# Two softmax attentions: eight PSUM banks shared out as 3, 4 and 1 in place of 4, 3 and 1

## The chip, the cores and the metric

One core of a Trainium2 chip runs the whole program in one launch. The metric is device time in microseconds (us): from the start to the end of one execution. Engines have short names: PE is TensorE (its matmuls), PEld is TensorE loading weights, DVE is VectorE, ACT is ScalarE, POOL is GpSimd, SP issues the DMAs.

## The reference, cut to what matters

The input x is (4, 512, 256) in fp32. Eight layers follow one another, each as `x = x + layer(layernorm(x))`. Two of them are softmax attentions with 16 heads of 16 channels; the other six (experts, two linear attentions, choosing experts) are not touched.

```python
def first_attention(x):                       # layer 1
    q, k, v = heads(x @ Wq.T), heads(x @ Wk.T), heads(x @ Wv.T)
    p = softmax(q @ k.T / sqrt(16))           # 512 x 512 for each head
    return merge(p @ v) @ Wo.T

def last_attention(x):                        # layer 7, causal
    ck = layernorm(x @ Wd.T) * gamma + beta   # 64 latent channels
    s = (heads(x) @ absorbed) @ ck.T / sqrt(16)
    p = softmax(where(query >= key, s, -inf))
    return merge(p @ (ck @ Wuv.T)) @ Wo.T
```

## The kernel before

**The work.** Both attentions are one function, `softmax_attention`. It has a prologue for the first batch entry and a loop of four turns, one for each batch entry. A turn has four head groups hg of four heads j; a group has four steps kt, one for each 128 keys. Scores are computed twice. The first pass (`scores`, L603) puts 128 queries on the partitions, so that DVE can take the maximum over the keys (`maximum`: L617, or L613 with the causal mask). The maxima are then folded into q (`negate_max`, `turn_max`, `put_max`). The second pass (`scores_t`, L724) puts 128 keys on the partitions and all queries on the 512 columns; ACT takes the exponential straight from PSUM (L840), and `values` (L739) multiplies by v. In step kt of group hg PE does the second pass of group hg and, in between, the first pass of the next group. In the causal attention matmuls, maxima and exponentials get narrower with kt or query tile, and POOL zeroes the masked corner of the exponentials (L915) before `values` may read them.

**Short names.** s0 to s3 are the first-pass scores of the four heads in a step, t0 to t3 the transposed ones, e0 to e3 their exponentials, V is `values` of the step before. A dash (t0') is the next step's. PE's order in a step is t0 t1, s3, V, s0, t2 t3, s1, [extras], s2. The extras belong to the finished group: its sums of exponentials in step 1 (`denominators`, L750) and its turned reciprocals in step 2 (`turn_reciprocals`, L759); group 2 has also the next entry's turned x and, in the causal layer, the latent projection. After the last step come the q and k of a later group (`qk`, eight passes or four), `turn_max` and V.

**TensorE.** An fp32 matmul is two passes over its columns. A score matmul has 32 rows (one head), so the four heads use four row groups of the array and can run side by side. V, `qk` and the extras use all 128 rows, and begin when the row groups have drained. PE takes its instructions in order: one that waits for a semaphore holds up all behind it.

**Banks.** Eight PSUM banks are handed out by rings (class `Ring`): whoever fills a ring's next bank waits on its `free` semaphore until the bank's last reader is done. Ring A has banks 0 to 3: q, k, v and the transposed scores. These are filled and read in pairs, and one exponential reads two banks (1024 columns). Ring D has banks 4 to 6: first-pass scores, the turned maxima, sums, reciprocals, turned x and latent tiles. Ring O has bank 7 for V's sum. The output projection writes into banks 2 and 3 (`y_banks`) at a turn's end; the wait on `y_free`, before v tile 2 of the next turn, is until DVE has added them to x.

So, when rings have n banks, a score may be filled when the one n places before it in the ring has been read.

Of the kernel before, what the change touches and what calls it, by code (L numbers as in the profile page):

```python
# [22 lines left out]
ACT = mybir.ActivationFunctionType  # L23
# [6 lines left out]
P = 128  # L30
B, T, DM = 4, 512, 256
NT = T // P
KD = DM // P
# [523 lines left out]
HG, HJ, DH, HP = 4, 4, 16, 32  # L557
# [3 lines left out]
def softmax_attention(nc, c, loads, w, causal):  # L561
# [4 lines left out]
    sb = c.carve(c.back, c.n7 if causal else c.n1)  # L566
    qs = sb("qs", [P, HG, T])
    ks = sb("ks", [P, HG, T])
# [3 lines left out]
    pt = sb("pt", [P, 4, 2, T])  # L572
# [5 lines left out]
    head_rows = [slice(j * HP, (j + 1) * HP) for j in range(HJ)]  # L578
# [1 line left out]
    first_slot = c.small[:, c.at["first_slot"]:c.at["first_slot"] + HJ]  # L580
    ones_row = c.small[:, c.at["ones_row"]:c.at["ones_row"] + 1]
    A, D, O = c.A, c.D, c.O
    D.take(c.banks[4:7])
    O.take(c.banks[7:8])
    max_uses = NT * HJ + 1
    y_banks = c.banks[2:4]

    def qk(pe, it, hg):
        pe.wait_ge(A.free.s, A.may_fill(it, 2))
# [3 lines left out]
    def keep_qk(act, it, hg):  # L593
        act.wait_ge(A.full.s, A.may_read(it, 2))
        nc.scalar.activation(qs[:, hg, :], A.read("q", hg)[:], ACT.Identity)
        nc.scalar.activation(ks[:, hg, :], A.read("k", hg)[:], ACT.Identity, bias=ones_row)\
            .then_inc(A.free.s, 2)
# [36 lines left out]
        bank = D.read("turn", hg)  # L634
        nc.vector.tensor_tensor(qs[:, hg, :], qs[:, hg, :], bank[:], ALU.add).then_inc(D.free.s, 1)  # L635

    A.open(4)
    D.open(w.extra_uses + max_uses, whole=False)
    c.first_step.open(w.links)
    c.max_ready.open(1)  # L640
# [2 lines left out]
    with nc.Block() as block:  # L643
        @block.tensor
        def _(pe):
            pe.wait_ge(c.s_small.s, 16)
            w.wait_weights(pe)
            pe.wait_ge(c.set_up.s, c.set_up.at(0, 2))
            pe.wait_ge(D.free.s, D.all_free(0))
            w.project_latent(pe, 0)  # L650
            w.turn_latent(pe, 0)
            qk(pe, 0, 0)
            qk(pe, 0, 1)
            pe.wait_ge(A.free.s, A.released(0, "k", 0))
            for qi in range(NT):
                for j in MAX_ORDER:
                    scores(pe, 0, 0, qi, j)
            turn_max(pe, 0, 0, 1)
            pe.wait_ge(A.free.s, A.released(0, "k", 1))
            pe.wait_ge(D.free.s, D.released(0, "turn", 0))  # L660
# [37 lines left out]
    c.y_free.base += 1  # L698
    c.y_full.open(2)
    c.y_free.open(2)  # L700
    A.open(NT + HG * (2 + NT * HJ))
    D.open(KD + w.extra_uses + HG * (max_uses + 2))
    O.open(HG)
    c.xn_ready.open(1)
    c.max_ready.open(HG)
# [5 lines left out]
    with nc.Block() as block:  # L711
        @block.tensor
        def _(pe):
            with pe.Fori(0, B) as it:
                def v_tile(i):
                    pe.wait_ge(A.free.s, A.may_fill(it))
                    w.v(A.fill("v", i)[:, 0:DM], i).then_inc(A.full.s, 1)

                def scores_t(hg, kt, pair):
                    q0 = kt * P if causal else 0  # L720
                    pe.wait_ge(A.free.s, A.may_fill(it, 2))
                    for j in (2 * pair, 2 * pair + 1):
                        bank = A.fill("s", hg, kt, j)
                        mm = nc.tensor.matmul(bank[:, q0:T], ks[head_rows[j], hg, kt * P:(kt + 1) * P],  # L724
                                              qs[head_rows[j], hg, q0:T], start=True, stop=True)
                    mm.then_inc(A.full.s, 2)

                def values(hg, kt):
                    q0 = kt * P if causal else 0
# [33 lines left out]
                def project(i, groups):  # L763

                    for hg in groups:
                        mm = nc.tensor.matmul(y_banks[i // 2][:, (i % 2) * DM:(i % 2 + 1) * DM],
                                              os_[:, hg, i * P:(i + 1) * P], w.wo[:, hg, :],
                                              start=(hg == 0 and i % 2 == 0), stop=(hg == HG - 1),
                                              skip_group_check=True)
                    return mm  # L770
# [12 lines left out]
                        w.turn_latent(pe, it)  # L783

                for i in range(NT):
                    if i == 2:
                        pe.wait_ge(c.y_free.s, c.y_free.at(it, 0))
                    v_tile(i)
                for hg in range(HG):
# [27 lines left out]
                for i in range(NT):  # L817
                    mm = project(i, range(HG - 1, HG))
# [5 lines left out]
        @block.scalar  # L824
        def _(act):
            with act.Fori(0, B) as it:
                for i in range(NT):
                    act.wait_ge(A.full.s, A.may_read(it))
                    bank = A.read("v", i)
                    nc.scalar.activation(v[:, i, :, 1:1 + DH], bank[:, 0:DM].rearrange("p (h d) -> p h d", d=DH),  # L830
                                         ACT.Identity).then_inc(A.free.s, 1)
                for hg in range(HG):
                    for kt in range(NT):
                        q0 = kt * P if causal else 0
                        for pair in range(2):
                            act.wait_ge(A.full.s, A.may_read(it, 2))
                            A.read("s", hg, kt, 2 * pair)
                            A.read("s", hg, kt, 2 * pair + 1)
                            two = c.a_pair[(A.r - 2) % 4 // 2]
                            nc.scalar.activation(pt[:, (kt % 2) * 2 + pair, :, q0:T], two[:, :, q0:T], ACT.Exp,  # L840
                                                 scale=0.25).then_inc(A.free.s, 2)
                    keep_qk(act, it, (hg + 2) % HG)
                    act.wait_ge(O.full.s, O.may_read(it))
                    bank = O.read("o", hg)
                    nc.scalar.activation(os_[:, hg, :], bank[:], ACT.Identity).then_inc(O.free.s, 1)
# [80 lines left out]
    if causal:  # L926
        c.sum_ready.close()
        c.kt_ready.close()
    c.set_up.base += 2


class MhaWeights:
# [10 lines left out]
    def memory(self, sb):  # L943
        pass
# [35 lines left out]
def mha_layer(nc, c, loads):  # L980
    softmax_attention(nc, c, loads, MhaWeights(nc, c), causal=False)
# [1108 lines left out]
class MlaWeights:  # L2090
# [21 lines left out]
    def memory(self, sb):  # L2112
        self.absorbed = sb("absorbed", [P, 512])
        self.ck = sb("ck", [P, NT, P])
        self.ct = sb("ct", [P, T])
        self.scratch = sb("scratch", [P, 3, T])
        self.spare = self.c.pool_spare

    def wait_weights(self, pe):
# [66 lines left out]
def mla_layer(nc, c, loads):  # L2186
    softmax_attention(nc, c, loads, MlaWeights(nc, c), causal=True)
# [265 lines left out]
```

## Time and profile before

| | us |
|---|---|
| median of 3 runs | 3036.81 (3034.34 to 3045.38) |
| the profiled execution | 3037.58 |
| its span, first to last instruction | 3035.7 |
| the first attention's loop, four turns | about 390 |
| the last attention's loop, four turns | about 398 |

Over the span PE is busy 91%, PEld 64%, DVE 52%, POOL 33% and ACT 29%. A busy PE is not a PE at its peak: a matmul's record covers its latency, and four row groups side by side count once. So the share of busy time doesn't tell whether the two loops could be shorter; the waits inside them do. The granted clock is a share of 2.4 GHz: 1.00 is that level, 0.50 is 1.2 GHz, and a stretch with both has a mean between. The record's own ends of matmuls are modelled, so the argument below goes by starts: weight loads are the sharpest marks on PE.

### The profile page before, as it was taken

Reading aid. Unit: us, or ns where it says so; the run is one execution under the profiler, and the core shown is the slowest. Engines: PE = TensorE matmul, PEld = TensorE weight load, DVE = VectorE, ACT = ScalarE, POOL = GpSimd, SP = SyncE. Lnnn points to the kernel's source line nnn. Section 1 sums busy time; section 2 is a strip of 40 time slices with the busy share of each in tenths; the row PEclk is TensorE's granted clock in tenths of the full one; section 3 lists DMA queues with packets and bytes.
Section 4 is the critical chain, followed back from the end, with each engine's and each line's share of the span. In section 5 each row is a group of like instructions: output and inputs, shape, how many; then the busy total and the mean of one; then the engine's idle time right before and its main releaser. Section 6 shows DMA issues by size and latency. Waiting matters only on the chain. (4 is left out here: it accounts for less than half of the span.)

```text
span 3035.7 us, 45759 instructions
## 1 busy us (share of the span) xinstructions
PE 2767.5 (91%) x15592; PEld 1930.3 (64%) x15592; DVE 1580.4 (52%) x4445; ACT 875.1 (29%) x1436; POOL 997.3 (33%) x1109
## 2 busy tenths in 40 slices
PE   7999999999999999999978999999999668888876
PEld 3434448887656566788867888888888543444444
DVE  4565545555755646455534333333334575555546
ACT  2444444443111101344432222222222002232310
POOL 0000017776544435576751122222221011122211
PEclk8999999999999999999989999999999658888975
DMA  3000020000000000200000000000000000000000
GB/s 144 1 0 0 0 91 14 0 0 0 1 0 0 0 0 0 84 1 0 0 14 1 15 15 15 15 1 15 15 1 1 25 0 1 1 0 1 0 0 28
DMA packets 6284, 37.92 MB, mean 12 GB/s; under 512 B 272, under 2 KB 4368, under 8 KB 4496
## 3 DMA queue, kind: packets, MB, share of 16 engines
q1 hardware_dynamic: 6160, 36.34, 3.1%
q8 instruction: 70, 1.15, 0.2%
q14 instruction: 54, 0.44, 0.0%
HBM read 34.24 MB, written 2.10 MB: 12 GB/s over the span
## 5 line engine op out<-in xcount | busy, mean ns | idle before, releaser
L603 PE MATMUL banks<-back 32*128 32x512 f32 (+3 forms) x1088 | 355.9, 583 | 30.1 <-DVE back L613 21.0
L365 PE MATMUL banks<-moe_parts 128*128 128x512 f32 x1536 | 366.7, 394 | 16.9 <-POOL moe_parts L471 10.4
L365 PEld LDWEIGHTS banks<-moe_parts 128*128 128x128 f32 x1536 | 286.0, 190 | 79.8 <-issue 22.5
L1447 PE MATMUL banks<-lin_parts 128*128 128x512 f32 x1152 | 307.3, 412 | 19.3 <-DVE lin_parts L1703 15.5
L840 ACT ACTIVATE back<-banks 128x1024 f32<-128x1024 f32 (+3 forms) x256 | 216.4, 863 | 292.6 <-PE banks L724 292.6
L1638 DVE TENSOR_TENSOR ffn_pack<-banks,back 128x512 f32<-128x512 f32 x128 | 88.5, 692 | 390.7 <-PE banks L1460 390.6
L1447 PEld LDWEIGHTS banks<-lin_parts 128*128 128x128 f32 x1152 | 211.9, 193 | 77.7 <-issue 31.2
L603 PEld LDWEIGHTS banks<-back 32*128 32x128 f32 x1088 | 130.5, 191 | 183.3 <-DVE back L617 77.8
L724 PE MATMUL banks<-back 32*128 32x512 f32 (+3 forms) x1024 | 233.3, 564 | 7.6 <-DVE back L635 3.3
L1768 POOL TENSOR_TENSOR ffn_pack<-ffn_pack 128x256 f32<-128x256 f32 x112 | 82.6, 738 | 456.7 <-ACT ffn_pack L1601 455.2
L617 DVE TENSOR_REDUCE back<-banks 128x1 f32<-128x512 f32 x272 | 176.5, 687 | 106.1 <-PE banks L603 101.1
L379 PE MATMUL banks<-moe_parts 128*128 128x256 f32 x1536 | 199.7, 286 | 5.3 <-POOL moe_parts L459 4.2
L379 PEld LDWEIGHTS banks<-moe_parts 128*128 128x128 f32 x1536 | 188.2, 191 | 24.4 <-issue 23.8
L520 DVE TENSOR_TENSOR moe<-moe,banks 128x512 f32<-128x512 f32 x128 | 87.5, 688 | 193.4 <-PE banks L365 190.9
L459 POOL TENSOR_TENSOR moe_parts<-moe,moe_parts 128x512 fp32r<-128x512 f32 x128 | 166.8, 1303 | 11.2 <-ACT moe_parts L416 11.2
L901 POOL TENSOR_TENSOR back<-back,small_pack 128x512 f32<-128x512 f32 x32 | 33.2, 1039 | 414.6 <-DVE back L856 414.6
L471 POOL TENSOR_TENSOR moe_parts<-ffn_pack,moe_parts 128x512 fp32r<-128x512 f32 x128 | 165.8, 1296 | 0.1
L1067 PE MATMUL banks<-xt,back 128*128 128x512 f32 x320 | 145.7, 598 | 1.7 <-PEq L336 1.7
L426 ACT ACTIVATE moe<-banks 128x512 f32<-128x512 f32 x128 | 76.6, 598 | 241.7 <-PE banks L365 241.7
L530 DVE SCALAR_TENSOR_TENSOR x<-banks,moe,x 128x256 f32 x256 | 109.2, 478 | 55.0 <-PE banks L379 49.6
L1167 ACT ACTIVATE lin<-banks 128x512 f32<-128x512 f32 x64 | 38.2, 597 | 342.2 <-PE banks L1116 205.8
L1601 ACT ACTIVATE ffn_pack<-banks 128x256 f32<-128x256 f32 x128 | 49.2, 384 | 300.0 <-PE banks L1497 300.0
(234 smaller groups left out, 5108.3 us busy)
## 6 DMA issues: line engine op xcount, KB each, us to landing
back<-p_raw SPq DMA_DIRECT2D x8, 1024.0 KB, 4.8
back<-p SPq DMA_DIRECT2D x1, 7696.0 KB, 21.2
ffn_pack<-ffn SPq DMA_DIRECT2D x1, 6144.0 KB, 26.8
back<-p SPq DMA_DIRECT2D x1, 5152.0 KB, 15.0
back<-p SPq DMA_DIRECT2D x2, 1792.0 KB, 8.1
out<-x SPq DMA_DIRECT2D x1, 2048.0 KB, 7.5
x<-x_in SPq DMA_DIRECT2D x1, 1536.0 KB, 12.7
small_pack<-small SPq DMA_DIRECT2D x1, 619.0 KB, 5.0
```

The source lines that it names most:

```text
L365: mm = nc.tensor.matmul(bank[:], up[:, n % 2, a, which, kd, :], xp[:, b, kd, :], start=((a, b, kd) == (0, 0, 0)), stop=((a, b, kd) == (1, ...
L379: mm = nc.tensor.matmul(bank[:, (i % 2) * DM:(i % 2 + 1) * DM], hp[:, (e % 2) * FC + f, a, i * P:(i + 1) * P], dn[:, e % 2, b, f, :], star ...
L459: nc.gpsimd.tensor_tensor(hp[:, n % 4, 1, :], gate[:, n % 4, :], hp[:, n % 4, 0, :], ALU.subtract)\
L471: nc.gpsimd.tensor_tensor(up[:, n % 2, 1], w_up[:, (n + 2) % UNITS], up[:, n % 2, 0], ALU.subtract).then_inc(c.up_lo.s, 1)
L530: ins = nc.vector.scalar_tensor_tensor(out=c.x[:, it, i, :], in0=bank[:, (i % 2) * DM:(i % 2 + 1) * DM], scalar=wt[:, i, e:e + 1], in1=c.x ...
L603: nc.tensor.matmul(bank[:, 0:n], qs[head_rows[j], hg, qi * P:(qi + 1) * P], ks[head_rows[j], hg, 0:n], start=True, stop=True).then_inc(D.f ...
L617: ins = nc.vector.tensor_reduce(mx[:, qi, j:j + 1], bank[:], AX, ALU.max)
L724: mm = nc.tensor.matmul(bank[:, q0:T], ks[head_rows[j], hg, kt * P:(kt + 1) * P], qs[head_rows[j], hg, q0:T], start=True, stop=True)
L840: nc.scalar.activation(pt[:, (kt % 2) * 2 + pair, :, q0:T], two[:, :, q0:T], ACT.Exp, scale=0.25).then_inc(A.free.s, 2)
L1067: mm = nc.tensor.matmul(bank[:], w[:, kd, :], c.xt[:, kd, :], start=(kd == 0), stop=(kd == KD - 1))
L1447: mm = nc.tensor.matmul(bank[:], wp[:, a, m, kd, r * P:(r + 1) * P], xp[:, b, x, kd, :], start=((a, x, kd) == (0, 0, 0)), stop=((a, x, kd) ...
L1638: nc.vector.tensor_tensor(am[:, n % 2].rearrange("p h r i -> p h (r i)"), pair[:, :, 0:2 * CH], decay[:, units[w][0]].rearrange("p h r i - ...
```

## The change

Inside the two attentions ring A gets banks 0 to 2 and ring D banks 3 to 6; A gets its four banks back at the end of the function. With three banks a pair would not fit evenly, so transposed scores are filled one bank at a time, each with its own wait, and each exponential reads one bank (512 columns) and gives back one bank. The projection's banks become 1 and 2, and the wait until they have been added moves from before v tile 2 to before v tile 1. The causal layer's scratch tile for masked scores gets a fourth part.

```diff
-    D.take(c.banks[4:7])
+    A.take(c.banks[0:3])
+    D.take(c.banks[3:7])
     O.take(c.banks[7:8])
-    y_banks = c.banks[2:4]
+    y_banks = c.banks[1:3]
...
                 def scores_t(hg, kt, pair):
                     q0 = kt * P if causal else 0
-                    pe.wait_ge(A.free.s, A.may_fill(it, 2))
                     for j in (2 * pair, 2 * pair + 1):
+                        pe.wait_ge(A.free.s, A.may_fill(it))
                         bank = A.fill("s", hg, kt, j)
-                        mm = nc.tensor.matmul(bank[:, q0:T], ks[head_rows[j], hg, kt * P:(kt + 1) * P],
-                                              qs[head_rows[j], hg, q0:T], start=True, stop=True)
-                    mm.then_inc(A.full.s, 2)
+                        nc.tensor.matmul(bank[:, q0:T], ks[head_rows[j], hg, kt * P:(kt + 1) * P],
+                                         qs[head_rows[j], hg, q0:T], start=True, stop=True).then_inc(A.full.s, 1)
...
-                    if i == 2:
+                    if i == 1:
                         pe.wait_ge(c.y_free.s, c.y_free.at(it, 0))
                     v_tile(i)
...
-                        for pair in range(2):
-                            act.wait_ge(A.full.s, A.may_read(it, 2))
...
-                            nc.scalar.activation(pt[:, (kt % 2) * 2 + pair, :, q0:T], two[:, :, q0:T], ACT.Exp,
-                                                 scale=0.25).then_inc(A.free.s, 2)
+                        for j in range(HJ):
+                            act.wait_ge(A.full.s, A.may_read(it))
+                            bank = A.read("s", hg, kt, j)
+                            nc.scalar.activation(pt[:, (kt % 2) * 2 + j // 2, j % 2, q0:T], bank[:, q0:T], ACT.Exp,
+                                                 scale=0.25).then_inc(A.free.s, 1)
...
+    A.take(c.banks[0:4])
...
-        self.scratch = sb("scratch", [P, 3, T])
+        self.scratch = sb("scratch", [P, 4, T])
```

How this stands in the program: TensorE of the first attention, behind the first V of a turn, up to t1 of the step after. Each name banks0 to banks3 is two banks (banks0 is banks 0 and 1, and so on). The 32-row score matmuls stand as 128x512 here. Before:

```order
L603 MATMUL banks3<-back0 128x512 [waits d_free]
L724 MATMUL banks1<-back0 128x512 [waits a_free]
L724 MATMUL banks1<-back0 128x512
L601 REGISTER_ALU
L603 MATMUL banks2<-back0 128x512 [waits d_free]
L601 REGISTER_ALU
L603 MATMUL banks2<-back0 128x512 [waits d_free]
L721 REGISTER_ALU
L724 MATMUL banks0<-back0 128x512 [waits a_free]
L724 MATMUL banks0<-back0 128x512
```

The same place in the changed kernel, where all line numbers in this function are one higher:

```order
L604 MATMUL banks2<-back0 128x512 [waits d_free]
L725 MATMUL banks0<-back0 128x512 [waits a_free]
L723 REGISTER_ALU
L725 MATMUL banks1<-back0 128x512 [waits a_free]
L602 REGISTER_ALU
L604 MATMUL banks2<-back0 128x512 [waits d_free]
L602 REGISTER_ALU
L604 MATMUL banks3<-back0 128x512 [waits d_free]
L723 REGISTER_ALU
L725 MATMUL banks0<-back0 128x512 [waits a_free]
L723 REGISTER_ALU
L725 MATMUL banks0<-back0 128x512 [waits a_free]
```

The order of the matmuls is the same (s0, t2, t3, s1, s2, t0', t1'). What moved is the waits: each t has its own, with a register computed for it, and the banks behind every wait are others.

ScalarE at the first step of the first attention, before:

```order
L836 REGISTER_ALU
L840 ACTIVATE back0<-banks0 128x1024 [waits a_full]
L836 REGISTER_ALU
L840 ACTIVATE back0<-banks1 128x1024 [waits a_full]
L836 REGISTER_ALU
```

And in the changed kernel:

```order
L838 ACTIVATE back0<-banks0 128x512 [waits a_full]
L836 REGISTER_ALU
L838 ACTIVATE back0<-banks1 128x512 [waits a_full]
L836 REGISTER_ALU
L838 ACTIVATE back0<-banks0 128x512 [waits a_full]
L836 REGISTER_ALU
L838 ACTIVATE back0<-banks0 128x512 [waits a_full]
```

Two exponentials a step have become four of half the width, and the fourth comes back to the bank of the first.

## Rows read from the trace of the kernel before

**Rows 1.** Windows: engines' busy time and granted clock in the two loops.
```profile
core 0: us, PE busy (x) PEld busy (x) DVE busy (x) ACT busy (x) POOL busy (x), PEclk, DMA share, GB/s
...
43.85:434.00 390.15, 381.36 (x2136) 171.86 (x2136) 218.96 (x437) 163.64 (x192) 16.62 (x16) 0.99 0.00 0
...
2536.00:2934.00 398.00, 345.31 (x2133) 167.89 (x2132) 217.30 (x1074) 121.27 (x191) 86.79 (x272) 0.89 0.00 1
```

**Rows 2.** Waits of one turn, first attention: waiter, releaser, us, times, longest.
```profile
PEld banks L603 <- DVE back L617: 17.9, 30, 1.0
```

**Rows 3.** Waits of one turn, last attention.
```profile
PEld banks L603 <- DVE back L613: 14.6, 17, 5.0
```

**Rows 4.** Timeline, PEld, same turn: start us, us, line, [idle before <-releaser].
```profile
151.33 0.16 PEld L739 LDWEIGHTS banks<-back 128*32 128x32 f32 x8 [0.76 <-ACT back L840]
...
155.28 0.16 PEld L739 LDWEIGHTS banks<-back 128*32 128x32 f32 x8 [0.76 <-ACT back L840]
...
159.23 0.16 PEld L739 LDWEIGHTS banks<-back 128*32 128x32 f32 x8 [0.76 <-ACT back L840]
...
166.21 0.16 PEld L739 LDWEIGHTS banks<-back 128*32 128x32 f32 x8 [0.17 <-issue]
...
171.02 0.16 PEld L739 LDWEIGHTS banks<-back 128*32 128x32 f32 x8 [0.76 <-ACT back L840]
...
174.08 0.19 PEld L724 LDWEIGHTS banks<-back 32*128 32x128 f32 x2
...
174.52 0.29 PEld L603 LDWEIGHTS banks<-back 32*128 32x128 f32 x2
175.57 0.16 PEld L739 LDWEIGHTS banks<-back 128*32 128x32 f32 x8 [0.76 <-issue]
...
176.57 0.19 PEld L724 LDWEIGHTS banks<-back 32*128 32x128 f32 x2
...
178.47 0.18 PEld L603 LDWEIGHTS banks<-back 32*128 32x128 f32 x1 [0.42 <-DVE back L617]
178.55 0.19 PEld L724 LDWEIGHTS banks<-back 32*128 32x128 f32 x2
...
180.11 0.16 PEld L739 LDWEIGHTS banks<-back 128*32 128x32 f32 x8 [0.76 <-issue]
...
187.38 0.16 PEld L739 LDWEIGHTS banks<-back 128*32 128x32 f32 x8 [0.17 <-issue]
```

**Rows 5.** Timeline, ACT, of the step that begins at 175.57.
```profile
177.84 1.02 ACT L840 ACTIVATE back<-banks 128x1024 f32<-128x1024 f32 x1 [1.47 <-PE banks L724]
```

**Rows 6.** Timeline, all engines, the beginning of that turn.
```profile
143.97 3.62 PE L975 MATMUL banks<-back,xt 128*128 128x256 f32 x16
...
144.28 0.69 DVE L891 TENSOR_TENSOR x<-x,banks 128x512 f32 x1 [0.17 <-PE banks L766]
...
147.52 0.19 PEld L724 LDWEIGHTS banks<-back 32*128 32x128 f32 x2 [0.33 <-ACT back L830]
...
148.75 1.94 ACT L840 ACTIVATE back<-banks 128x1024 f32<-128x1024 f32 x2 [0.73 <-PE banks L724]
```

**Rows 7.** Groups by form, ACT, one turn: count, busy us, mean ns.
```profile
L845 ACT ACTIVATE back<-banks 128x512 f32<-128x512 f32 x4 | 2.4, 597 | 1.2 <-PE banks L739 1.2
```

**Rows 8.** Timeline, PEld and ACT, first step of a group, last attention.
```profile
2761.01 0.16 PEld L739 LDWEIGHTS banks<-back 128*32 128x32 f32 x8 [1.16 <-POOL back L915]
...
2758.39 1.94 ACT L840 ACTIVATE back<-banks 128x1024 f32<-128x1024 f32 x2 [1.06 <-PE banks L724]
```

**Rows 9.** Last attention, group 2: PEld timeline, then a window with its clock.
```profile
2792.62 0.50 PEld L603 LDWEIGHTS banks<-back 32*128 32x128 f32 x2 [4.99 <-DVE back L613]
2794.19 0.71 PEld L759 LDWEIGHTS banks<-small_pack,back 128*128 128x128 f32 x4 [1.07 <-DVE back L613]
...
2786.50:2810.00 23.50, 17.74 (x67) 6.39 (x66) 12.84 (x59) 3.31 (x7) 2.18 (x8) 0.57 0.00 0
```

**Rows 10.** Timeline, DVE, the first attention's prologue.
```profile
33.69 1.43 DVE L617 TENSOR_REDUCE back<-banks 128x1 f32<-128x512 f32 x2 [0.49 <-PE banks L603]
```

More of the change, by code:

```diff
@@ L635, in put_max @@
         nc.vector.tensor_tensor(qs[:, hg, :], qs[:, hg, :], bank[:], ALU.add).then_inc(D.free.s, 1)
-    A.open(4)
+    A.open(4, whole=False)
     D.open(w.extra_uses + max_uses, whole=False)
@@ L700, in softmax_attention @@
     c.y_free.open(2)
-    A.open(NT + HG * (2 + NT * HJ))
-    D.open(KD + w.extra_uses + HG * (max_uses + 2))
+    A.open(NT + HG * (2 + NT * HJ), whole=False)
+    D.open(KD + w.extra_uses + HG * (max_uses + 2), whole=False)
     O.open(HG)
@@ L834, in _ @@
                         q0 = kt * P if causal else 0
-                        for pair in range(2):
-                            act.wait_ge(A.full.s, A.may_read(it, 2))
-                            A.read("s", hg, kt, 2 * pair)
-                            A.read("s", hg, kt, 2 * pair + 1)
-                            two = c.a_pair[(A.r - 2) % 4 // 2]
-                            nc.scalar.activation(pt[:, (kt % 2) * 2 + pair, :, q0:T], two[:, :, q0:T], ACT.Exp,
-                                                 scale=0.25).then_inc(A.free.s, 2)
+                        for j in range(HJ):
[3 more added lines that the diff above has]
+                                                 scale=0.25).then_inc(A.free.s, 1)
                     keep_qk(act, it, (hg + 2) % HG)
```

## The prediction

> **What bounds the kernel now.** I read the windows first. The change touches the two attention loops: 390 us and 398 us of 3036, about 97.5 and 99.5 us for each of their four turns [rows 1]. ACT, whose work the change cuts up, is busy 164 of 390 us and 121 of 398; PE is the engine with least room. Then the waits of one turn: in the first attention PE stands 17.9 us of 97.5 before first-pass scores, 30 times, until DVE has read a bank of ring D [rows 2]; in the last one 14.6 us [rows 3]. The chain that ended last is of no use here: it runs through the layer behind the attentions. The timeline of weight loads then shows a step as a row of marks, V to V: 3.95 us in group 0 (155.28 to 159.23), 4.81 for a group's first step (166.21 to 171.02), 4.55 and 4.54 for those with sums or reciprocals between (171.02, 175.57, 180.11), then 7.27 with q and k [rows 4]. I take step by step what comes last before V.
>
> A step's fixed parts, all between starts. From V to the next loads (X): 1.00 (175.57 to 176.57). From X to the exponential of what was loaded there: 1.27 (176.57 to 177.84) [rows 4, 5]; on idle row groups at a group's start 1.23 (147.52 to 148.75) [rows 6]. From the last score load, s3', to V: 1.05 (174.52 to 175.57) [rows 4]. From a reader's end to the load that it frees: 0.05, a round value. Behind a load that has waited, the next waiting load comes 0.08 later (178.47 to 178.55); I use 0.07 [rows 4].
>
> **Ring D, four banks for three.** s2 now waits for the s2 of the step before, not for s3 of its own step; s3' for s3, not s0. Extras in between count as fills. These waits end last in the steps with extras: with reciprocals the load of s2 stands 0.42 us at 178.47, and s3' after it waits again [rows 4]. In the changed kernel those releases are a whole fill older, and the wait is gone. What is late next is ring A.
>
> **Ring A, three single banks for four in pairs.** A t may be filled when the one three places before has been read: t1' waits for e2, t0' for e1, t2 for e3 of the step before, t3 for e0 of its own step. An exponential of one bank is 0.60 (another ACT operation of 512 columns reading one bank: 597 ns [rows 7]) against 1.02 for a pair [rows 5]. On ACT two in a row of 1.02 take 1.94 [rows 6], an overlap of 0.10, so I let short ones follow each other by 0.50. The critical path of a plain step becomes: X, e2 begins at X+1.27, ends X+1.87, t1' loads at X+1.92, s3' at X+1.99, V at X+3.04, next X at +4.04.
>
> The Trainium skill speaks against the smaller exponentials. ScalarE: Activation LUTs, in the section What ACT_TABLE_LOAD costs, gives an ACTIVATE a fixed 186 ns beside 0.833 ns for each column, so halving pays the fixed part twice. The trace agrees: 2 x 0.60 is 0.18 over 1.02 [rows 5, 7]. By the rule alone 256 pairs (32 a turn) would cost 256 x 0.19 = 48 us; by the trace a plain step has 2.4 us of exponentials in 4 us, so that cost lies beside PE's work.
>
> **The sum for a turn of the first attention.**
> - Two plain steps in group 0: 4.04 for 3.95, +0.18.
> - Three steps with sums (171.02 to 175.57): t0', t1' load at 174.08 anyway, and e2 is over by then (X+1.92 = 173.94). s3' loads at 174.09 for 174.52: -0.43 each, -1.29.
> - Three with reciprocals (175.57 to 180.11): t1' at 176.57+1.92 = 178.49, s3' at 178.56, V at 179.61 for 180.11: -0.50 each, -1.50.
> - Steps with q and k: 6.98 in three of four, where PE never waits; the one at 187.38 took 7.27 since DVE was late: -0.29.
> - First steps of groups 1 and 3: t3 waits for e0 (X+1.88), s1 and s2 queue behind it; t1' follows e2, which begins 1.00 after e0: X+2.88; s3' +0.07; V at X+4.00, the step 5.00 for 4.81: +0.19 each, +0.38. Group 2's, 6.00 with its turned x, I take as unmoved.
> - Beginning of the turn: V came 3.81 after the first load (147.52 to 151.33) and now 4.00 as above: +0.19 [rows 4, 6]. The new place of the y wait: v tile 1 would load at 143.97+0.86 (a quarter of 16 passes in 3.4 us) = 144.83, but x is added at 144.28+0.69+0.05 = 145.02: +0.19 [rows 6].
>
> Together -2.15, four times: -8.6. The bounds: below, all 17.9 us of ring D's waits go and ring A costs nothing (-72); above, ring A's losses alone (+0.75 a turn, +3). I stand near the upper end, since each gain was followed to the next wait.
>
> **The last attention.** Maxima are narrow here, so DVE frees ring D early in a group, and ring A's loss shows whole. First step: the two pairs' exponentials run back to back from 2758.39 to 2760.33, then POOL's mask, then V at 2761.01 [rows 8]. With three banks t3 loads at 2758.39+0.60+0.05 = 2759.04, e3 begins 1.23 later and ends at 2760.87: +0.54. Twice: +1.1. At the turn's beginning the same and the y wait: +0.74. In group 2 the turned x stands behind the late t3 (about 1.5 later than now); between 0.54 and that whole delay I take +0.9, as PE had some slack there. Gains: three steps where s2 waits about 0.5 for DVE (14.6 us less one of 4.99, over 16 waits [rows 3, 9]): -1.5. In group 2 DVE normalises the latent, and s1 waits 4.99 us for a bank, until 2792.62; the reciprocals follow at 2794.19 [rows 9]. With a fourth bank s1 has gone before, and the reciprocals load at 2792.62: -1.57. The granted clock is 0.57 there, a mixture of the two levels 2.4 and 1.2 GHz. If PE gets 2.4 GHz back at the old time, half comes back: -0.8. The larger scratch tile adds no instruction. Sum +0.45 a turn, +1.8 in all. Bounds: -14.6 (all waits) and +2.7 (the losses alone) a turn.
>
> **Prologues.** DVE is held up by ring D: gaps like the 0.49 at 33.69 [rows 10] sum to 2.2 us in the first one. The loop that follows has a clock of 0.99, not 1.00 [rows 1]: its first few us run at 1.2 GHz still, and an earlier start has more of them, which gives half back: -1.1; for the last attention I take half of that, -0.5: -1.6. From 0 to -3.3.
>
> Total -8.6 + 1.8 - 1.6 = -8.4 on the profiled execution's 3037.58 us (0.8 above the median): 3029.
>
> **Rivals.**
> 1. *Ring A is never last* (0.08). If a bank comes free sooner than I think, plain steps fall to PE's own 1.00 and twice 1.05, 3.1, and those with reciprocals to 3.5 (0.71 for the transposes at half speed [rows 9]): -0.85 x 2 - 1.05 x 3 - 1.29 - 0.29 = -6.4 a turn. For it: ACT idles 1.6 us in a plain step. Against it: t1' cannot precede e2, a chain of 1.92. 3037.6 - 25.7 - 1.6 = 3010.
> 2. *The trade cancels* (0.17). Loads that wait cost more than 0.07 each, or first steps lose more; what ring D gives in six steps of a turn, ring A takes in the others. 3033 to 3042, most likely 3037.
> 3. *ACT's queue* (0.07). The place is e2: if ACT is still at e1 when t2 is done, e2 begins 0.50 later, and every step that ends with t1' grows by 0.50: two plain, three with reciprocals, four first ones, +4.5 a turn in the first attention, +2 in the last. -8.6+18+1.8+8-1.6 = +17.6: 3055. It decides once e1 ends after X+1.27. By my chain t1 loads 2.12 before X, so e1 ends at X-0.25, which leaves 1.5 us.
>
> **How the numbers follow.** My forecast, 0.68, is 3029, its own range 3022 to 3035. About 0.5% (15 us) is what a measurement can tell from no change: faster is below 3021.6, slower above 3052. Faster is rival 1 and a tail of 0.07 of the forecast: 0.15. Slower is rival 3 and 0.01: 0.08. The rest is 0.77. The range 3019 to 3040 takes in rival 2 and leaves out rivals 1 and 3.
>
> **What would show it.** Right: V to V of 4.0 in plain steps and with reciprocals, 4.1 with sums, 5.0 for first steps; loads of first-pass scores hardly waiting for DVE, transposed ones waiting for ACT instead; the first attention's turn at 95.4, the last's near 99.5 or above. Wrong: plain steps near 3.4 (ring A not last) or 4.5 (ACT's queue); the last attention's first steps unmoved; another length of its stretch at half speed, which alone is worth a few us.

## The result, and the profile after

| | before | after |
|---|---|---|
| median of 15 runs each, us | 3035.50 (3033.47 to 3046.43) | 3048.93 (3047.44 to 3052.90) |
| ratio, 95% interval | | 1.0040 [1.0031, 1.0049] |
| profiled span, us | 3035.7 | 3048.6 |

The kernel became slower by 13 us in medians; the forecast was 3029, and its range ended at 3040. (Executions of several kernels here, the one before among them, lie in two groups some 10 us apart, which is why ranges are wide; the loops below are read from one profiled execution each.)

Where the 12.9 us of span are, is read by cutting both traces at the first and the last V of each loop. Windows of the kernel before, first attention and last:

```profile
53.71:425.57 371.86, 363.87 (x2055) 159.47 (x2054) 215.53 (x432) 158.39 (x184) 15.58 (x15) 1.00 0.00 0
2542.80:2925.39 382.59, 332.12 (x2062) 158.46 (x2062) 213.16 (x1056) 116.60 (x185) 84.61 (x267) 0.89 0.00 1
```

The same of the changed kernel, and the last attention again by its four turns:

```profile
56.37:417.82 361.45, 356.40 (x2055) 157.32 (x2054) 214.75 (x432) 166.93 (x310) 15.61 (x15) 1.00 0.00 0
2535.76:2938.80 403.04, 352.44 (x2062) 168.63 (x2062) 213.19 (x1058) 125.94 (x310) 84.31 (x267) 0.84 0.00 1
...
2535.76:2635.54 99.78, 85.80 (x536) 42.81 (x536) 54.52 (x271) 32.73 (x81) 21.55 (x68) 0.92 0.01 1
2635.54:2737.85 102.31, 88.72 (x536) 43.59 (x536) 54.19 (x271) 32.83 (x81) 21.62 (x68) 0.87 0.00 0
2737.85:2846.21 108.36, 94.96 (x536) 46.12 (x537) 54.60 (x271) 33.05 (x81) 21.62 (x68) 0.81 0.00 0
2846.21:2938.80 92.59, 82.96 (x454) 36.11 (x454) 49.87 (x251) 27.33 (x70) 19.53 (x63) 0.74 0.00 0
```

These answer to [rows 1]. The first loop became 10.4 us shorter, the last 20.4 us longer. The first V came 2.7 us later, between the loops lie 0.7 us more, and behind them 0.5 less. In the last loop DVE and POOL did the same work as before and ACT 9 us more, while PE's clock fell from 0.89 to 0.84, and from turn to turn it falls further (0.92, 0.87, 0.81, 0.74). Before, the turns took 102.0, 99.2, 99.1 and 82.4 us: the first turn became 2.2 us shorter, the others 3.2, 9.3 and 10.2 longer. The granted clock adds up to 85 us at 1.2 GHz in this loop before, and 133 us after. The stretch behind group 2's 5 us wait even became shorter in every turn (17.1 us to 13.7, then three times 20.5 to 17.1); new are three long stretches that begin in a group's first step, of 10.2, 23.9 and 23.9 us. In all, 48 us more at half speed are worth up to 24 us.

The waits of one turn in the first attention, changed kernel (waiter, releaser, us, times, longest):

```profile
PEld banks L604 <- DVE back L618: 10.1, 15, 0.8
...
PEld banks L725 <- ACT back L838: 4.6, 9, 0.7
```

And of one turn in the last one:

```profile
PEld banks L604 <- DVE back L614: 7.4, 12, 1.2
...
PEld banks L759 <- DVE back L614: 5.0, 1, 5.0
...
PEld banks L725 <- ACT back L838: 4.1, 8, 0.7
```

Against [rows 2, 3], ring D's waits fell from 17.9 to 10.1 and from 14.6 to 7.4 us; transposed scores wait for ACT instead. Of the 15 waits left in the first attention 11 are the 0.84 behind V (as at 152.50 below). That gap stands at 160.46 too, where no releaser is found, so it is hardly a wait for a bank, before or after. In the last attention 5.0 of the 7.2 us did not go: the wait behind DVE's latent has moved from a first-pass score to the reciprocals (L759).

Weight loads of the first attention, a plain step and a group's first three steps, the places of [rows 4]:

```profile
151.50 0.16 PEld L739 LDWEIGHTS banks<-back 128*32 128x32 f32 x8 [0.76 <-ACT back L838]
152.50 0.18 PEld L604 LDWEIGHTS banks<-back 32*128 32x128 f32 x1 [0.84 <-DVE back L618]
154.35 0.18 PEld L725 LDWEIGHTS banks<-back 32*128 32x128 f32 x1 [0.69 <-ACT back L838]
155.48 0.16 PEld L739 LDWEIGHTS banks<-back 128*32 128x32 f32 x8 [0.76 <-ACT back L838]
...
166.44 0.16 PEld L739 LDWEIGHTS banks<-back 128*32 128x32 f32 x8 [0.17 <-issue]
...
169.25 0.18 PEld L725 LDWEIGHTS banks<-back 32*128 32x128 f32 x1 [0.66 <-ACT back L838]
...
171.36 0.16 PEld L739 LDWEIGHTS banks<-back 128*32 128x32 f32 x8 [0.76 <-ACT back L838]
...
175.48 0.16 PEld L739 LDWEIGHTS banks<-back 128*32 128x32 f32 x8 [0.76 <-issue]
...
179.46 0.16 PEld L739 LDWEIGHTS banks<-back 128*32 128x32 f32 x8 [0.76 <-ACT back L838]
```

A plain step is 3.98 us (151.50 to 155.48), with the wait of t1' for e2 at 154.35, 1.85 behind X. The group's first step is 4.92, the one with sums 4.12, with reciprocals 3.98.

The last attention where the clock is lost, second turn, from the end of group 0 into group 1. Windows of the changed kernel: the step with q and k, the next group's first step up to the fall and from it on, the step with sums:

```profile
2642.38:2647.70 5.32, 4.49 (x27) 1.77 (x26) 4.19 (x22) 1.62 (x4) 0.85 (x3) 1.00 0.00 0
2647.70:2651.68 3.98, 3.24 (x29) 2.03 (x30) 1.37 (x8) 2.27 (x5) 0.55 (x2) 1.00 0.00 0
2651.68:2652.86 1.18, 1.13 (x5) 0.15 (x2) 1.07 (x9) 0.90 (x3) 0.55 (x2) 0.50 0.00 0
2652.86:2659.71 6.85, 6.84 (x32) 3.02 (x33) 2.09 (x12) 1.64 (x5) 2.13 (x5) 0.50 0.00 0
```

The same steps of the kernel before:

```profile
2651.77:2657.08 5.31, 5.19 (x27) 1.86 (x26) 4.02 (x20) 1.04 (x3) 0.68 (x3) 1.00 0.00 0
2657.08:2661.86 4.78, 3.38 (x31) 1.76 (x30) 2.96 (x19) 3.56 (x5) 1.09 (x4) 1.00 0.00 0
2661.86:2665.55 3.69, 3.69 (x32) 1.75 (x32) 1.28 (x9) 1.10 (x3) 1.31 (x5) 1.00 0.00 0
```

The step with sums takes 6.85 us at 1.2 GHz for 3.69. What PE did up to the fall at 2651.68 and just behind it stands in its weight loads, changed kernel:

```profile
2644.49 0.30 PEld L2176 LDWEIGHTS banks<-xt,back 128*128 128x128 f32 x2 [1.01 <-ACT back L838]
...
2647.11 0.42 PEld L630 LDWEIGHTS banks<-small_pack,back 128*128 128x128 f32 x4 [1.47 <-DVE back L614]
...
2650.43 0.18 PEld L725 LDWEIGHTS banks<-back 32*128 32x128 f32 x1 [0.66 <-ACT back L838]
...
2651.41 0.18 PEld L725 LDWEIGHTS banks<-back 32*128 32x128 f32 x1 [0.20 <-ACT back L838]
...
2652.86 0.20 PEld L739 LDWEIGHTS banks<-back 128*32 128x32 f32 x8 [1.03 <-POOL back L913]
```

Four waits stand ahead of the fall: a q or k pass for its bank in ring A (1.01 for 0.76 before), the turned maxima for DVE (1.47 for 0.94), then t3 and t1' for exponentials (0.66 and 0.20; before, t0' alone waits there, 0.39). V's wait for POOL lies behind the fall (1.03 for 1.16).

These waits alone do not decide a fall. In group 1 of the changed kernel t3 waits the same 0.66 us in all four turns (2552.19, 2650.43, 2752.74, 2862.71); the clock fell in the second and the fourth turn and held in the first and the third. Here is the first step and the step with sums of the third turn, then of the fourth:

```profile
2749.99:2755.18 5.19, 3.89 (x31) 2.13 (x30) 2.45 (x16) 3.45 (x8) 1.10 (x4) 1.00 0.00 0
2755.18:2758.87 3.69, 3.69 (x32) 1.75 (x32) 1.79 (x12) 1.04 (x4) 1.33 (x5) 1.00 0.00 0
...
2859.98:2865.53 5.55, 4.60 (x31) 2.54 (x30) 2.45 (x16) 3.37 (x7) 1.10 (x4) 0.80 0.00 0
2865.53:2872.38 6.85, 6.85 (x33) 3.02 (x33) 2.09 (x12) 1.50 (x5) 2.13 (x5) 0.50 0.00 0
```

### The profile page after: what moved, and what is told of

The parts are those of the page before. It is cut to its first block and busy times, and to the rows that moved or that the text cites. A ratio compares the mean times of both kernels' runs of the same rounds, so it can differ in the third digit from the quotient of the medians.

```text
span 3048.6 us, 46275 instructions
## 1 busy us (share of the span) xinstructions
PE 2779.9 (91%) x15592; PEld 1939.0 (64%) x15592; DVE 1577.9 (52%) x4445; ACT 894.3 (29%) x1692; POOL 997.8 (33%) x1109
## 3 DMA queue, kind: packets, MB, share of 16 engines
q8 instruction: 71, 1.16, 0.2%
## 5 line engine op out<-in xcount | busy, mean ns | idle before, releaser
L365 PE MATMUL banks<-moe_parts 128*128 128x512 f32 x1536 | 366.4, 394 | 16.8 <-POOL moe_parts L471 10.4
L604 PE MATMUL banks<-back 32*128 32x512 f32 (+3 forms) x1088 | 341.6, 605 | 5.8 <-DVE back L2173 4.5
L838 ACT ACTIVATE back<-banks 128x512 f32<-128x512 f32 (+3 forms) x512 | 234.8, 516 | 284.6 <-PE banks L725 283.4
L725 PE MATMUL banks<-back 32*128 32x512 f32 (+3 forms) x1024 | 280.4, 587 | 10.6 <-DVE back L636 5.3
L618 DVE TENSOR_REDUCE back<-banks 128x1 f32<-128x512 f32 x272 | 175.6, 685 | 102.5 <-PE banks L604 99.2
L604 PEld LDWEIGHTS banks<-back 32*128 32x128 f32 x1088 | 127.3, 199 | 118.6 <-DVE back L618 44.1
L725 PEld LDWEIGHTS banks<-back 32*128 32x128 f32 x1024 | 108.6, 196 | 62.9 <-ACT back L838 35.0
```

What stands on the lines that cost most here:

```text
L365: mm = nc.tensor.matmul(bank[:], up[:, n % 2, a, which, kd, :], xp[:, b, kd, :], start=((a, b, kd) == (0, 0, 0)), stop=((a, b, kd) == (1, ...
L604: nc.tensor.matmul(bank[:, 0:n], qs[head_rows[j], hg, qi * P:(qi + 1) * P], ks[head_rows[j], hg, 0:n], start=True, stop=True).then_inc(D.f ...
L618: ins = nc.vector.tensor_reduce(mx[:, qi, j:j + 1], bank[:], AX, ALU.max)
L838: nc.scalar.activation(pt[:, (kt % 2) * 2 + j // 2, j % 2, q0:T], bank[:, q0:T], ACT.Exp, scale=0.25).then_inc(A.free.s, 1)
```

## The experiments

The letters of the theories are those of the expectations. All kernels but the two that were compared are the changed one with a table for the first attention (`False`) and the last (`True`): banks of rings A and D, one bank an exponential or two, whether the prologue has four and three banks, and where extra matmuls stand, whose result is overwritten. Each takes the identity times k into the next bank that its ring has free:

```diff
+PLAN = {False: dict(a=3, d=4, single=True, pro4=False, fill=()),
+        True: dict(a=3, d=4, single=True, pro4=False, fill=())}
...
+                def busy(ring, hg, times, n):
+                    pe.wait_ge(ring.free.s, ring.may_fill(it))
+                    bank = ring.banks[len(ring.labels) % len(ring.banks)]
+                    for _ in range(times):
+                        nc.tensor.matmul(bank[:, 0:n], c.ident, ks[:, hg, 0:n], start=True, stop=True)
...
+                    if "max" in fill:
+                        busy(D, after, 1, T)
                     turn_max(pe, it, after, hg + 1)
                     values(hg, NT - 1)
+                    if "put" in fill and hg + 1 < HG:
+                        busy(A, hg, 1, 2 * P)
```

Measured, with the loops from V to V in the profiled execution and the granted clock's time at 1.2 GHz in the last one. Each ratio is to runs of the kernel before that were taken beside it; their medians were 3044.4 us with e1 to e4, 3035.0 with e5 to e8 and 3038.2 with e9 to e12.

| run | median, us | ratio to before [95%] | first loop | last loop | at 1.2 GHz |
|---|---|---|---|---|---|
| before | 3035.5 | | 371.9 | 382.6 | 85 |
| after | 3048.9 | 1.0040 [1.0031, 1.0049] | 361.5 | 403.0 | 133 |
| e1 change in the first only | 3024.9 | 0.9952 [0.9933, 0.9971] | 361.5 | 382.6 | 85 |
| e2 change in the last only | 3070.8 | 1.0087 [1.0060, 1.0115] | 371.9 | 403.0 | 133 |
| e3 four-bank prologues | 3054.5 | 1.0053 [1.0033, 1.0074] | 361.5 | 408.7 | 150 |
| e4 both fills | 3037.9 | 0.9985 [0.9969, 1.0001] | 361.5 | 387.1 | 72 |
| e5 last: A 3, D 3 | 3088.7 | 1.0169 [1.0146, 1.0191] | 361.5 | 441.8 | 208 |
| e6 last: A 4, D 3, singles | 3031.5 | 0.9983 [0.9963, 1.0003] | 361.5 | 384.0 | 82 |
| e7 fill before maxima alone | 3075.4 | 1.0132 [1.0101, 1.0162] | 361.5 | 422.6 | 157 |
| e9 fill behind values alone | 3035.0 | 0.9980 [0.9965, 0.9995] | 361.5 | 385.4 | 82 |
| e8 first changed, last filled | 3014.7 | 0.9929 [0.9912, 0.9946] | 361.5 | 371.0 | 31 |
| e10 both changed, three fills | 3021.4 | 0.9939 [0.9916, 0.9962] | 361.4 | 375.6 | 27 |
| e11 e8 with more fill | 3029.9 | 0.9957 [0.9939, 0.9975] | 361.5 | 373.7 | 21 |
| e12 before, with e8's fill | 3030.2 | 0.9968 [0.9948, 0.9988] | 372.0 | 370.9 | 31 |

By their medians e1 (3 us below) and e9 came about as expected; e4, e6, e10 and e12 lie 1 to 4 us above the expected range, e8 7, e2 14, e11 16, and e3, e5 and e7 9 to 34. The loops of e1, e2, e4, e6, e9, e10 and e12 came where they were expected. So the argument goes by loops and clock, and not by totals.

The last loop has eight places of one kind: the first steps of groups 1 and 3 in four turns. By the granted clock a new fall begins there, or in the step behind, 0 times in the kernel before, e1 and e6, 3 times in the changed kernel and e2, 4 times in e3 and e5, 6 times in e7, once in e8, e9 and e12, and for a short stretch once in e11 and twice in e4 and e10.

**The two attentions apart.**

```diff
-        True: dict(a=3, d=4, single=True, pro4=False, fill=())}
+        True: dict(a=4, d=3, single=False, pro4=False, fill=())}
```

> The change in the first attention only; the last attention has its four banks for first-pass scores in pairs of exponentials, and three for the others, as in the kernel before. Theory C (the last attention's extra time comes from half-speed stretches that its own 3-4-1 sharing brings on) and theory W (from the waits on ring A themselves): the first attention's loop stays at 361 us where it was 372, its prologue at +2.7, the last attention's loop returns from 403 to about 382, and the time is 3035.5 - 10.4 + 2.7 = 3028 us. Theory P (the half-speed stretches depend on when the loop starts, not on how it shares its banks): the last attention keeps part or all of its 20 us, 3036 to 3048.

e2 has that line for `False` in place of `True`.

> The change in the last attention only, the first one as before. Theories C and W: the last loop takes 403 us as in the changed kernel, the first 372, and the time is 3035.5 + 20.5 + about 1 = 3057 us, the slowest of the four. Theory P: the last loop starts some 10 us later than in the changed kernel and may take anything from 382 to 403: 3036 to 3057.

Windows of e1, both loops:

```profile
55.52:416.99 361.47, 356.42 (x2055) 157.54 (x2054) 214.84 (x432) 166.88 (x310) 15.59 (x15) 1.00 0.00 0
2533.57:2916.18 382.61, 332.51 (x2062) 158.53 (x2062) 213.51 (x1055) 116.23 (x185) 83.90 (x267) 0.89 0.00 1
```

And of e2:

```profile
54.90:426.82 371.92, 363.94 (x2055) 159.74 (x2054) 215.53 (x432) 158.35 (x184) 15.59 (x15) 1.00 0.00 0
2555.96:2958.99 403.03, 352.38 (x2062) 168.80 (x2062) 213.28 (x1058) 125.89 (x310) 84.13 (x267) 0.84 0.00 1
```

e1's last loop began 2 us earlier than in the changed kernel and took the 382.6 of before; e2's began 20 us later and took the 403.0 of after, with stretches of the same length at half speed in the same steps. So theory P falls: the 20 us belong to the sharing in the last attention. And the change is worth 10 us in the first one. (e2's median lies 13.8 us above the expected 3057; 12 of them its profiled execution has between the loops, 2129 us for 2117, where no line differs, and one of its five runs took 3058.6.)

**The prologues.**

```diff
-PLAN = {False: dict(a=3, d=4, single=True, pro4=False, fill=()),
-        True: dict(a=3, d=4, single=True, pro4=False, fill=())}
+PLAN = {False: dict(a=3, d=4, single=True, pro4=True, fill=()),
+        True: dict(a=3, d=4, single=True, pro4=True, fill=())}
```

> The change in both loops, but the q, k and v projections ahead of each loop use four banks of ring A and three of ring D as before. If the prologue's loss is the third bank's missing neighbour (2.61 us of wait for ACT at the second q and k pair), the first values group returns from 56.4 to 53.7 us, and the last attention's prologue gains as much or less: 3048.9 - 2.7 to 5 = 3044 to 3046 us. If it is something else, 3049.

The second pair of q and k in the first prologue, timeline of PE, changed kernel:

```profile
26.77 3.68 PE L962 MATMUL banks<-xt,back 128*128 128x512 f32 x4 [2.61 <-ACT back L597]
```

It waits 2.61 us for ACT to read the first pair; with four banks (before) it starts at 22.98 without a wait. All seven profiled kernels with three banks there have this wait, and none of the seven with four. In e3 it is gone and the first V is at 53.78 for 56.37. The wait is shown, its price only roughly: over the seven with three banks the first V lies from 53.4 to 56.5 (middle one 56.0), over the seven with four from 53.4 to 54.9 (middle one 53.9), since the clock rises and falls at different moments of the prologue. And the time rose: the last loop, which began 4.4 us earlier, got a further 20.5 us at half speed in its first turn, at a step that held the clock in the changed kernel with the same waits, and took 5.7 us longer. The total was a miss: where the clock stands on an edge, what is saved ahead of it can be lost again.

**Keeping PE busy.**

```diff
-        True: dict(a=3, d=4, single=True, pro4=False, fill=())}
+        True: dict(a=3, d=4, single=True, pro4=False, fill=('max', 'put'))}
```

> The change in both attentions, and in the last one extra matmuls whose result is overwritten: one of 128 x 512 before the maxima are turned, one of 128 x 256 behind a group's last values, so that TensorE works where it stood waiting for DVE or ACT. Theory C: the half-speed stretches that are new in turns 5 to 7 vanish, the last loop returns to 380 to 388 us, and the time is 3028 to 3034. Theory W: the waits were not the clock's, the extra work of 0.2 us and 0.1 us lies in them at best, and the time stays at 3046 to 3055.

e7 has `('max',)`, e9 `('put',)`.

> The change in both attentions, with one extra matmul of 128 x 512, whose result is overwritten, ahead of the turned maxima in the last one, and none behind a group's last values. If the wait ahead of the turned maxima decides the clock (1.5 us where it was 0.9), the last loop is at 385 to 390 us as with both fills, and the time at 3033 to 3040. If the wait of the next group's first step decides, it stays at 400 or more: 3045 to 3055.

> The change in both attentions, with one extra matmul of 128 x 256, whose result is overwritten, behind a group's last values in the last one, and none ahead of the turned maxima. The changed kernel's last loop took 403.1 us without either, 422.7 with the one ahead of the maxima alone, 387.1 with both. If the wait of a group's first step is the one that decides the clock, this one alone brings the loop to 383 to 390 us and the time to 3028 to 3038. If it takes both, 398 us or more, 3043 and above.

Windows of e9, fourth turn: the first step of group 1 with the extra matmul in it, and the step with sums, to be set beside the fourth turn of the changed kernel above:

```profile
2855.47:2860.70 5.23, 4.27 (x34) 2.42 (x33) 2.44 (x16) 3.46 (x7) 1.09 (x4) 1.00 0.00 0
2860.70:2864.39 3.69, 3.69 (x33) 1.75 (x34) 1.80 (x12) 1.04 (x4) 1.34 (x5) 1.00 0.00 0
```

The waits for exponentials are still there (0.66 and 0.20, at 2858.26 and 2859.23) and the first step is still 5.23 us. But PE has work in the whole of its first 1.5 us, for 1.0 in the changed kernel, the clock holds, and the step with sums is 3.69 for 6.85. Theory W, by which the waits themselves cost the 20 us, falls. One matmul of 128 x 256 behind a group's last V gives back 17.6 of 20.4 us: both new stretches of 23.9 us are gone, the one of 10.2 in the second turn stays. Both fills give no more (387.1).

Two things keep this from being a full account. The wait that is filled, 0.50 us for the folded maxima, stands in the kernel before too (at 2658.01): the fill makes up for the new wait of t3 and does not remove it. And no run moved these steps in time without giving PE work, so that a mere shift by the fill's 0.07 us is not excluded, though all three kernels with this fill (e4, e9, e10) have at most 82 us at half speed and the others with 3, 4 and 1 banks there at least 133. The fill ahead of the maxima, alone, was worse than none (422.6 for 403.0): the expectation's second branch, 400 or more, did not say that, and its 3045 to 3055 missed the 3075; why is not settled.

**Which ring.**

```diff
-        True: dict(a=3, d=4, single=True, pro4=False, fill=())}
+        True: dict(a=3, d=3, single=True, pro4=False, fill=())}
```

> The change in the first attention; in the last one three single banks for transposed scores as in the change, but three for first-pass scores as before (one bank of eight unused). Theory A (the falls to half speed come of ring A's third bank, which makes a group's first step 0.4 to 0.5 us longer in one piece): the last loop stays at about 400 us and the new half-speed stretches are there: 3045 to 3055. Theory D (they come of ring D's fourth bank, which lets first-pass scores run ahead, so that the whole wait for DVE's maxima stands in one piece ahead of the turned maxima): the new stretches are gone, the last loop takes 382.6 plus ring A's losses of 2 to 4 us: 3027 to 3030.

e6 has `a=4, d=3`.

> The change in the first attention; in the last one ring A with four banks and ring D with three as before, but transposed scores released and exponentials taken bank by bank. Smaller exponentials alone: four banks cover the later release, so theory A and theory D both expect the last loop within 3 us of the 382.6 that it takes with pairs: 3023 to 3028. If the smaller exponentials themselves are the cause (ACT's fixed cost twice, so that the masks and the sums come later), the new half-speed stretches are here too: 3040 or more.

Weight loads of e5 at a group's first step, from the first transposed score that waits to the next V:

```profile
2552.26 0.18 PEld L739 LDWEIGHTS banks<-back 32*128 32x128 f32 x1 [0.66 <-ACT back L875]
2553.24 0.28 PEld L739 LDWEIGHTS banks<-back 32*128 32x128 f32 x1 [0.20 <-ACT back L875]
2554.81 0.20 PEld L763 LDWEIGHTS banks<-back 128*32 128x32 f32 x8 [0.99 <-POOL back L950]
```

And of e6:

```profile
2652.49 0.18 PEld L739 LDWEIGHTS banks<-back 32*128 32x128 f32 x1 [0.19 <-ACT back L875]
2654.09 0.16 PEld L763 LDWEIGHTS banks<-back 128*32 128x32 f32 x8 [1.23 <-POOL back L950]
```

The two differ in one bank of ring A, with which the projection's banks and the place of the wait for them move. With three, t3 waits 0.66 us for e0 and the clock falls at 2553.3, and so in group 1 of all four turns; with four it holds there in all four, and the loop is 57.9 us shorter. Theory A holds, though the loop came out 40 us longer than it expected: going from four banks to three in ring A brings the falls on. It is not the only thing that can: e8 and e12, with four banks in pairs, have one new stretch of 10.2 us behind a group's first step in their third turn. Exponentials of one bank cost 1.4 us in the loop (384.0 for 382.6), 0.35 a turn. Theory D was not only wrong but turned round: from three to four banks, ring D gives 39 us back (441.8 to 403.0).

**A faster kernel.** In the kernel before, each turn's long stretch of half speed begins in the 4.99 us of [rows 9] (in the first turn at 2591.7, for a score that loads at 2593.19). Six extra matmuls stand ahead of the score that waits there; the first attention has the change, with a four-bank prologue:

```diff
-PLAN = {False: dict(a=3, d=4, single=True, pro4=False, fill=()),
-        True: dict(a=3, d=4, single=True, pro4=False, fill=())}
+PLAN = {False: dict(a=3, d=4, single=True, pro4=True, fill=()),
+        True: dict(a=4, d=3, single=False, pro4=False, fill=('latent6',))}
...
+                        if "latent6" in fill and (hg, kt) == (2, 2):
+                            busy(A, hg, 6, T)
                         scores(pe, it, after, kt, MAX_ORDER[2])
```

> The change in the first attention, with four and three banks in its prologue; the last attention as before the change, and in group 2's third step, ahead of the first-pass scores that wait 4.99 us for a bank, six extra matmuls of 128 x 512 whose result is overwritten. Without them the time would be 3024.9 - 2.6 = 3022 us. Theory C: they fill about 3 of the 5 us, TensorE keeps the higher clock there, and in each turn most of the 17 to 20 us at half speed behind that wait is gone, which gives back 4 to 8 us a turn: 2990 to 3008. If the clock falls there for another reason, 3022 to 3026; if the fills come late and hold up the scores, 3026 to 3035.

e12 has this fill in the kernel before.

> The kernel before in both attentions, with six extra matmuls of 128 x 512 (result overwritten) in the last one, in group 2's wait of 4.99 us. Theory C: what the fill gave beside the change in the first attention it gives alone: the last loop at about 371 us for 382.6, 3035 - 11.6 = 3023 us, 3020 to 3028. If the loop's start decides, 3028 to 3040.

e8's fill in PE's timeline, with the score behind it:

```profile
2574.73 5.42 PE L750 MATMUL banks<-back,small_pack 128*128 128x512 f32 x12
2580.08 0.91 PE L613 MATMUL banks<-back 32*128 32x384 f32 x2
```

Windows of e8, the step with reciprocals and the next:

```profile
2573.11:2582.75 9.64, 9.64 (x41) 3.86 (x40) 8.11 (x43) 1.37 (x3) 1.09 (x4) 1.00 0.00 0
2582.75:2591.70 8.95, 7.35 (x32) 2.95 (x31) 3.97 (x16) 0.91 (x3) 1.09 (x4) 0.81 0.01 3
```

The same two in the kernel before:

```profile
2587.11:2597.82 10.71, 6.33 (x29) 2.19 (x28) 8.20 (x43) 1.41 (x3) 1.09 (x4) 0.71 0.00 0
2597.82:2609.24 11.42, 10.29 (x31) 3.73 (x30) 3.94 (x16) 0.88 (x3) 1.09 (x4) 0.52 0.00 1
```

5.42 us of useless matmuls make these two steps of the first turn 3.54 us shorter. e12 shows the same 371 us without the change, so this gain and that of the first attention add up: 11.6 and 10.4 of the profiled spans' 24.1 (3035.7 to 3011.6). The expectation for e8 had twice the gain, 4 to 8 us a turn for 2.9. In part that is a misreading: I took a record of 0.48 us for a matmul, but one is two passes, so six filled 5.4 us, not 3, and ran over; the score behind them loads 6.96 us behind V, for 6.08. That is 0.9 us a turn; the rest of the miss is not traced.

```diff
-                            busy(A, hg, 6, T)
+                            busy(A, hg, 8, T)
...
-                    if "put" in fill and hg + 1 < HG:
+                    if "put0" in fill and hg == 0:
```

> The version of 3014.7 us (change in the first attention with four and three banks in its prologue, last attention as before with six extra matmuls in the wait of group 2) with eight of them and one of 128 x 256 behind the last values of group 0. Eight take about 3.9 us of the wait of 4.99. Theory C: the stretches of 10.2, 6.8 and 3.4 us at half speed that were left (30.7 in all) go in part: 3005 to 3014. If the eight hold up the scores behind them, 3015 to 3022.

With that mistake the eight take 7.13 us: the step with reciprocals grew from 9.64 to 11.37, and the loop is 2.7 us longer than e8's, with less half speed. (The medians lie 15 us apart, the profiled spans 3.7: 3015.3 for 3011.6.)

```diff
-        True: dict(a=3, d=4, single=True, pro4=False, fill=())}
+        True: dict(a=3, d=4, single=True, pro4=False, fill=('max', 'put', 'latent'))}
...
+                    if "latent" in fill and hg == 2 and kt == 2:
+                        busy(A, hg, 6, T)
                     if hg and kt == 2:
                         turn_reciprocals(hg - 1)
```

> The change in both attentions, four and three banks in the prologues, and in the last attention extra matmuls (results overwritten) at three waits: ahead of the turned maxima, behind a group's last values, and six of 128 x 512 ahead of the reciprocals that wait for DVE in group 2. Theory C: the last loop has little half speed left (under 40 us of it), 365 to 378 us, and the time is 3007 to 3020. If 3, 4 and 1 banks are also the better sharing there once the clock holds, this is below the 3014.7 of the version with the last attention as before; if the longer first steps (5.2 for 4.8 us) eat it, above.

e10 also has the four-bank prologue, in the first attention only. With nearly the same time at half speed (27 and 31 us), 3, 4 and 1 banks take 375.6 us in the last attention and 4, 3 and 1 take 371.0. Its first steps (5.23 for 4.78, in group 2 5.72 for 4.78) and the turn's beginning (17.47 for 16.65) outweigh what ring D gives; e10's two further fills have a share in this that was not measured apart. The fastest kernel is e8, 20 us below the kernel before.

## Why the prediction was wrong, point by point

- **First attention, -8.6: right.** It was -10.4, -2.5 a turn for -2.15, and not by luck: every step came within 0.08 us (measured, then forecast): plain 3.98 (4.04), sums 4.12 (4.12), reciprocals 3.98 (4.04), first steps 4.92 (5.00), q and k 6.98 (6.98), group 2's first 6.03 (6.00); the turn's beginning lost 0.48 for 0.38. Rivals 1 and 3 fall: neither 3.4 nor 4.5 occurs, and t1' waits for e2 in place.
- **Last attention, +1.8: the step that failed.** At the higher clock its steps came as forecast: group 2's step with reciprocals 9.13 for 10.71 (-1.58, forecast -1.57), its first step +0.88 (+0.9), the other reciprocals -0.54 (-0.5), first steps +0.39 (+0.54), the turn's beginning +0.83 (+0.74). What failed is the clock term. I let the clock change only in the stretch that was there, "half comes back", and named "another length of its stretch at half speed, which alone is worth a few us" as what could prove me wrong, with no price in the sum or the range. The old stretches did become shorter; what the term left out is that new ones begin elsewhere. The loop measured +20.4 for +1.8. The runs show four things: the sharing in the last attention brings it (e1, e2), three banks in ring A in place of four bring the falls on (e5, e6), the time is lost at 1.2 GHz in the steps behind (6.85 for 3.69 us), and work for PE at a group's start gives most of it back (e9). That t3's wait for e0 is the link between the bank and the fall is argued, since the same wait stands in turns where the clock held. The stretches before ([rows 1], clock 0.89) said that this loop was near the edge: four long ones, one from each 5 us wait. The Trainium skill tells of such a kernel in TensorE: Matmul & The Clock Gate, section A second HAM failure mode: psum-queue depth-cycling: one that cycled through PSUM banks, in bf16, idled so often in small pieces between groups of matmuls that the clock went back and forth. This trace agrees so far: no single wait ahead of the fall at 2651.68 is above 1.47 us.
- **Prologues, -1.6: wrong in sign, +3.4 in the two profiled executions.** I counted only ring D's waits there. Ring A feeds q and k too, and with three banks it adds a wait of 2.61 us (e3). The size is uncertain by about as much as the term: the first V moves by 3 us among kernels with the same prologue.
- **Rival 2** (the trade cancels, 3037) saw a wrong place: ring A takes little back in the first attention (0.03 us in a plain step, 0.11 in a first step, 0.48 at a turn's beginning). No rival had the clock.

Open: which of the eight places loses the clock in a given turn, how a fourth bank of ring D takes 75 of e5's 208 us at 1.2 GHz away, and why e7's fill made it worse.

## What to carry to other kernels

Where the granted clock already falls in a loop, a new wait of half a microsecond is not priced by its length: read the windows' clock ahead of it, and give the range what a fall there would cost (here 3.2 us for one step of 3.7, and 9.5 for a group's four steps, 26.6 for 17.1). A loop shared by two layers of different shapes may need two plans for its banks: the same change was -10 us in one and +20 in the other. And a wait that can't be removed can be filled: 5.4 us of matmuls whose result nobody reads were worth 11.6 us of 383. They have to end about with the wait: 7.1 us of them gave less.

## What the runs showed of the hardware that was not expected

- PE's busy share in the profile does not tell where the clock falls. In e5 the last 3.78 us before the fall have 3.03 of PE busy; in e6 the whole first step has 3.59 of 4.83, a smaller share, and there the clock holds.
- Neither do the waits. The same step with the same waits lost the clock in two of four turns of the changed kernel (1.00 in the third turn, 0.80 in the fourth).
- A matmul of 128 x 512 in fp32 shows as two records, 5.42 us for twelve at 2.4 GHz, so counts of records are not counts of matmuls.
